# A planned order by longest path, more filling matmuls, and one matmul for a step of a recurrence

## The reference

```
attn_a: q,k,v = x@W_qkv.T + b;  gains = softmax(q@W_qscale.T + scale_gain)   # 16 heads of 8, 11 scales
        out += gains[j] * D4[tau] * sum(q * shift(k, d*tau)) * shift(v, d*tau)  # d = 1,2,4..., tau = 0..3
        out += softplus(bypass) * sum(q*k) * v;  result = (out * sigmoid(x@W_gate.T + b)) @ W_out.T + b_out
ffn:    e = argmax(x@Wg.T) of 8 experts;  y = gelu(x@W1[e] + b1[e]) @ W2[e] + b2[e]
attn_b: h = tanh(h@A.T + (x@B.T)[t]);  y[t] = h@C.T  for t = 0..511;  layernorm(y + x)*gamma + beta
ffn:    as above, with the same weights
```

## Time and profile before

| | us |
|---|---|
| median of the runs (3) | 1426.97 |
| lowest, highest run | 1420.13, 1428.18 |
| span of the profiled execution | 1436.4 |
| PE busy in it | 1170.8 (82%) |
| DVE, ACT, POOL busy | 796.3, 651.3, 788.6 |
| mean granted PE clock | 0.858 |

### The profile page before, as it was taken

The page is one execution under the profiler, slowest core; times in us unless marked ns, Lnnn a source line. Parts: engine busy times, 40 slices in busy tenths (PEclk is TensorE's granted clock), DMA queues, the critical chain, the costliest instruction groups (busy, mean ns, idle before and its releaser), DMA issues. The chain is left out here.

```text
span 1436.4 us, 32831 instructions
## 1 busy us (share of the span) xinstructions
PE 1170.8 (82%) x9942; PEld 881.1 (61%) x9942; DVE 796.3 (55%) x1723; ACT 651.3 (45%) x2050; POOL 788.6 (55%) x1274
## 2 busy tenths in 40 slices
PE   3877886888888899789988899887899998995580
PEld 2644554566565666466655666676787777785570
DVE  4878788889966777576788647542122301240110
ACT  2233332465544664455554436363564344562250
POOL 2645458563776748862748844876315642324504
PEclk9989987999988998889999759788995567998895
DMA  4700001221221212111112221233332324444542
GB/s 126 213 1 0 1 1 47 61 65 58 86 66 44 64 44 70 51 51 38 44 46 86 60 63 46 77 97 105 108 104 77 98 83 123 118 132 121 146 116 60
DMA packets 117638, 107.58 MB, mean 75 GB/s; under 512 B 15540, under 2 KB 88541, under 8 KB 117469
## 3 DMA queue, kind: packets, MB, share of 16 engines
q1 hardware_dynamic: 106704, 88.01, 21.5%
q0 software_dynamic: 8192, 16.79, 3.9%
q10 hardware_dynamic: 2573, 0.69, 0.2%
HBM read 76.73 MB, written 28.70 MB: 73 GB/s over the span
## 5 line engine op out<-in xcount | busy, mean ns | idle before, releaser
L799 POOL TENSOR_TENSOR acc<-acc,term 128x512 f32<-128x512 f32 x219 | 281.5, 1286 | 71.9 <-DVE term L1341 54.8
L1160 PE MATMUL bank<-w,hT 128*128 x1088 | 217.5, 324 | 22.1 <-ACT hT L985 13.9
L1341 DVE TENSOR_TENSOR term<-bank,V 128x512 f32<-128x512 f32 x251 | 168.0, 684 | 67.2 <-PE bank L1110 44.0
L1005 ACT ACTIVATE hid<-bank 128x16 f32<-128x16 f32 x512 | 93.0, 182 | 243.6 <-PE bank L1187 203.0
L985 ACT ACTIVATE hT<-bank,b1T 128x128 f32<-128x128 f32 x544 | 165.2, 370 | 79.2 <-PE bank L1147 65.2
L839 POOL DMA_INDIRECT back<-sorted_y,slot_i x128 | 125.1, 978 | 135.8 <-DMA back<-sorted_y,slot_i 44.2
L1160 PEld LDWEIGHTS bank<-w,hT 128*128 128x128 f32 x1088 | 173.9, 221 | 41.1 <-issue 35.6
L1187 PEld LDWEIGHTS bank<-hid,abcT 128*32 128x32 f32 x4096 | 88.6, 116 | 162.2 <-ACT hid L1005 83.2
L1312 DVE SCALAR_TENSOR_TENSOR made<-bank,qkvb,K 128x512 f32<-128x512 f32 x251 | 176.2, 742 | 17.8 <-PE bank L1083 7.2
L1187 PE MATMUL bank<-hid,abcT 128*32 128x16 f32 x4096 | 138.6, 201 | 38.3 <-ACT hid L1005 37.1
L1147 PE MATMUL bank<-xTb,w1b 128*128 128x128 f32 x864 | 166.8, 321 | 3.2 <-ACT xTb L973 3.0
(11 more groups left out here) (177 smaller groups left out, 2153.4 us busy)
## 6 DMA issues: line engine op xcount, KB each, us to landing
w1b<-in_W SPq DMA_DIRECT2D x130, 256.0 KB
K<-in_W SPq DMA_DIRECT2D x54, 256.0 KB
xsb<-sorted_x SPq DMA_DIRECT2D x184, 64.0 KB
sorted_y<-ysb SPq DMA_DIRECT2D x136, 64.0 KB
X<-in_x SPq DMA_DIRECT2D x64, 64.0 KB
out_x<-X SPq DMA_DIRECT2D x64, 64.0 KB
sorted_x<-K SPq DMA_DIRECT2D x14, 256.0 KB, 3.6
sorted_y<-made SPq DMA_DIRECT2D x48, 64.0 KB
```

What stands on the lines that cost most here:

```text
L799: nc.gpsimd.tensor_tensor(acc[:], acc[:] if k > 1 else term[0][:], term[k % NTERM][:], ALU.add).then_inc(S["terms_added"], 1)
L1005: nc.scalar.activation(hid[n % 2][:, cs], bank[6 + n % 2][:, cs], ACT.Tanh).then_inc(S["h_ready"], 1)
L1160: last = nc.tensor.matmul(bank[SLOT_BANK[place(n)]][:, 0:D], tile(hT[place(n)], c), w2[:, ds(second[n] + c * D, D)], start=(c == 0), stop= ...
L1341: V_.tensor_tensor(term[k % NTERM][:], bank[2 + k % 2][:], V[:, at:at + CW], ALU.mult).then_inc(S["terms_ready"], 1)
```

## The change

Three things change; the computation does not.

1. The planner's durations are replaced by pairs (how soon the engine can take the next piece, when the result is there), with a delay by pair of engines. The choice goes by the longest path that still hangs on a piece, instead of the earliest start.
2. The filling rule: every planned gap may be filled, at 0.11 us a matmul, as many as bring the planned columns of a stretch up to a target. There are 1916 fillers in place of 486, and bank 0 may take them too.
3. A step of the recurrence is one matmul of 128 rows.

```diff
-    def piece(engine, what, n, k, us, rank, after, lands=0.15, bank0=None):
-        us = us * PE_PACE if engine == "PE" else us
+PACE = dict(
...
+    rows=(0.42, 0.60), rxb=(0.93, 1.06), ry=(0.92, 1.06), step=(0.22, 0.33), turn=(0.12, 0.27), xT=(0.45, 0.60),
...
+    rnorm=(0.38, 0.48), rnorm2=(0.38, 0.48), xnorm=(0.38, 0.48), rcopy=(0.49, 0.58), rxcopy=(0.49, 0.60), state=(0.08, 0.18),
...
+HOP = {("ACT", "PE"): 0.13, ("ACT", "DVE"): 0.03, ("PE", "ACT"): 0.05, ("PE", "DVE"): 0.04, ("DVE", "PE"): 0.06, ("DVE", "ACT"): 0.03}
...
-            piece("PE", "step", c, k, 0.28, URGENT,
-                  [("state", c, k - 1) if k else past("state", c - 1, CT - 1), ("rxb", c, 0) if k == 0 else None])
+            piece("PE", "step", c, k, [("state", c, k - 1) if k else past("state", c - 1, CT - 1), ("rxb", c, 0) if k == 0 else None])
...
-                choice = (at, todo[key][2], ready, key)
...
+        to_go[key] = max((hop(todo, key, y) + to_go[y] for y in followers[key]), default=todo[key].took)
...
+            if r <= now + LOOK_US:
+                choice = (DAWDLE * max(0.0, r - now) - to_go[key], key)
...
+SPAN_US, TARGET, FILL_US, FILL_COLS, FREE_US = 3.4133, 6000, 0.11, 256, 0.3
...
-        if best and end and BEGIN[key] - best[0] > IDLE_US:
-            out[key] = int((BEGIN[key] - best[0]) * FILL_SHARE / FILL_US), best[1], best[2]
+        lack = TARGET - sum(c for _, c in recent) - columns_of(*key)
+        most = int((at - since) / FILL_US)
+        if end and lack > 0 and most > 0:
+            late = sum(since + FILL_US * j > stop - SPAN_US for j in range(most))
+            times = most - late + min(late, -(-lack // FILL_COLS))
...
-                    if reader:
+                    if reader and b == 0:
+                        pe.wait_ge(S["bank0_taken"], filled)
+                    elif reader:
...
-                    for q in range(4):
-                        last = nc.tensor.matmul(bank[6 + u][32 * q:32 * q + 32, k * NB:(k + 1) * NB],
-                                                abcT[:, 32 * q:32 * q + 32], prev, start=False, stop=True,
-                                                skip_group_check=True)
-                    last.then_inc(S["step_psum"], 1)
+                    nc.tensor.matmul(bank[6 + u][:, k * NB:(k + 1) * NB], abcT[:, 0:D], prev, start=False, stop=True,
+                                     skip_group_check=True).then_inc(S["step_psum"], 1)
```

More of the change, by code:

```diff
@@ new lines, in cost @@
+def cost(what, n, k):
+    if what in ("hidden", "result"):
+        us = 0.222 * HC / parts(n)
+        return us, us + 0.17
+    if what == "gelu":
+        us = 0.25 * HC / parts(n)
+        return us, us + 0.12
+    if what == "spread" and terms(n)[k].g not in (0, 1):
+        return 0.87, 1.02
+    if what == "spread":
+        return 0.31, 0.47
+    if what == "scale" and k == 2:
+        return 0.21, 0.31
+    if what == "xmom" and STATS_GROUP[n][1] - STATS_GROUP[n][0] == 1:
+        return 3.16, 3.17
+    return PACE[what]
@@ L192, in past, with pieces, piece @@
+def pieces():
+    todo = {}
+    def piece(engine, what, n, k, after, bank0=None):
+        todo[what, n, k] = Piece(engine, *cost(what, n, k), [x for x in after if x is not None], bank0)
     def past(what, n, k=0):
         return (what, n, k) if n >= 0 else None
-    URGENT, USUAL = 0.0, 1.0
     for i in range(CHUNKS):
@@ L282, in timeline @@
-        piece("DVE", "resid", i, 0, 0.7, USUAL, [("out", i, 0)], bank0=0)
+                piece("POOL", "add", i, j, [("term", i, j), ("add", i, j - 1) if j > 1 else None, past("out", before)])
+        piece("PE", "gatep", i, 0, [("xcopy", i, 0), past("gate", before)], bank0=1)
+        piece("ACT", "tanh", i, 0, [("gatep", i, 0)], bank0=0)
+        piece("DVE", "gate", i, 0, [("add", i, n - 1), ("tanh", i, 0)])
+        piece("PE", "out", i, 0, [("gate", i, 0)], bank0=1)
+        piece("DVE", "resid", i, 0, [("out", i, 0)], bank0=0)
@@ L359, in timeline @@
+        piece("PE", "rxb", c, 0, [("rxcopy", c, 0)])
         for k in range(CT):
[L360 to L365 removed]
@@ L376, in timeline @@
-    engines = ["SP", "POOL", "ACT", "PE", "DVE"]
-    left = {key: len(x[3]) for key, x in todo.items()}
+            piece("PE", "step", c, k, [("state", c, k - 1) if k else past("state", c - 1, CT - 1), ("rxb", c, 0) if k == 0 else None])
+            piece("ACT", "state", c, k, [("step", c, k), past("ry", c - 2) if k == 0 else None])
+        piece("PE", "ry", c, 0, [("state", c, CT - 1)])
+        piece("DVE", "rres", c, 0, [("ry", c, 0)])
+        piece("DVE", "rstats2", c, 0, [("rres", c, 0), past("rmom2", c - 2)])
@@ new lines, in pieces, with hop @@
+        piece("POOL", "rmom2", c, 0, [("rstats2", c, 0), past("rnorm2", c - 2, TPC - 1)])
+        for k in range(TPC):
+            piece("ACT", "rnorm2", c, k, [("rmom2", c, 0), ("rnorm2", c, k - 1) if k else None])
+        piece("DVE", "rgam", c, 0, [("rnorm2", c, TPC - 1)])
+        piece("DVE", "rbeta", c, 0, [("rgam", c, 0)])
+        piece("DVE", "rout", c, 0, [("rbeta", c, 0)])
+    return todo
+def hop(todo, x, y):
+    e, f = todo[x].engine, todo[y].engine
+    return todo[x].took + HOP_OF.get((x[0], y[0]), HOP.get((e, f), 0.08)) + LANDS.get(x[0], 0.0)
@@ L430, in fillings @@
+CLOSED_BY = dict(xT="xcopy", kproj="kcopy", vproj="vcopy", logit="shift", rows="rcopy", reduce2="pack2", gatep="tanh", out="resid",
+                 pT="pcopy", plog="plg", counts="ccopy")
 def fillings():
[L433 to L434 removed]
+    out, end, recent = {}, None, []
+    last_of = {b: None for b in range(8)}
     for key in ORDER["PE"]:
         what, n, k = key
+        at, stop = BEGIN[key], BEGIN[key] + WORK[key].pace
         best = None
[L438 to L439 removed]
+        for b, x in last_of.items():
+            since = max(end or at, BEGIN[x] + WORK[x].took + FREE_US) if x else end or at
```

314 lines of the change are left out of this document (162 added, 152 removed).

## The result

| | before | changed |
|---|---|---|
| median of the runs | 1425.43 (4 runs) | 1320.78 (4 runs, 1314.4 to 1323.52) |
| ratio to before, 95% interval | | 0.9285 [0.9224, 0.9346] |
| span of the profiled execution | 1436.4 | 1321.6 |
| mean granted PE clock | 0.858 | 0.950 |

A forecast was written before the change was run, and what follows sets the result against it. No engine is full; chains of small pieces waiting in in-order queues, chiefly the stream of slots, set the end. Terms -70 - 25 - 15 - 33 + 15 = -128 took 1427 to 1299 us, range 1195 to 1425.

The forecast's parts named there:

- order, waits and clock: Slots beside attention -70 us, PE's waits for states -25, the half-clock stretch of 19 slots behind attention -15.
- fillers: 1430 more matmuls in PE's gaps hold the clock: -10, -15 and -8 us in three stages, together -33.
- the step: One 128-row matmul per recurrence step: half of 16 us PE time, plus 7 us for later results, +15 us.
- a possible 140: Most the two stretches of 23 slots beside attention could save at the third's 5.3 us a slot: 81 and 59 us.
- my bound of 37: Most the half-clock stretch of 19 slots could save: 139 us down to 102 at 5.3 us a slot.
- My bound of 120: Most that PE's waits in front of states could return, from a row of 120.3 us in 161 waits.
- a microsecond at half clock in which PE sets the pace: Fillers' term: worth 0.4 us each, so at most 32, 52 and 26 us in three stages.
- Rival 3: Array shape costs on the way into a step too: step's term -8 instead of +15, 1276 us; chance 0.11.
- My estimate of 213 ns: Two weight loads of 128 columns by the skill's rule, near the 0.22 us forecast for a new step's hold.
- The signs given: Trace readings named beforehand to show the forecast right or wrong: slot stretches, state waits, clock, step timings, attention's end.
- Rival 1: The order returns nothing, since a better plan slips too; only fillers and step remain, 1409 us; chance 0.15.
- Rival 4: Recurrence put off into half clock: 267 steps behind attention's end at 1.66 us each, 1450 us; chance 0.12.

The follow-up runs named there:

- the pair of kernels on one chip: Kernel before with only the new filling rule, 1423.76 us, against the changed kernel with the old step of four 32-row matmuls, 1352.52 us.
- the first two kernels of the third chip: Changed kernel without the 447 fillers behind the last spread, 1402.88 us; changed kernel with its planner's step hold at 0.15 instead of 0.22 us, 1402.83 us.

## Why the prediction was right, and where it was not

The ledger predicted -110 for order, waits and clock, -33 for fillers, +15 for the step, -128 in all. Measured: order with its fillers -71 on one chip, step -32 against the changed kernel on others, together -103.

**Order: -70, -25 and -15 us, with -33 for fillers, measured -71 together.** Each mechanism is there, and in its own view larger than I took it. In the pair of kernels on one chip, the stretches of 23 slots beside attention are 98 us shorter from first to last transpose, of a possible 140. The 19 slots behind attention are 25 us shorter there; the 54 us of the result, over my bound of 37, compare with a trace that holds 11 us of "remote" waits and 92 us at half clock in this stretch, and the old order took 104 us for it, not 118, where those waits were missing. The wait for states fell by 61 us, counted once. My bound of 120 for it was wrong by its reading: the row of 120.3 us adds the waits of weight loads and of matmuls, which lie inside each other, so that 83 us was all there was. The last job, for which I took nothing from the order, gave 19 us. The end came forward by 71 us only. These are views of one chain of time, not separate savings: PE's waits are part of what made the slots long. Adding them to each other and to the fillers made the sum for order and fillers, 143 us, twice what was measured. That the sum of -128 came near -105 is in part luck: this overcount and the wrong sign of the step's term offset each other.

**Fillers: -33.** In the new order they are worth 46 us: 27 and 25 us in the first two stages (I took 10 and 15), and 1 and -4 in the others, where I took 8 for the last job. The 46 us are those of all 1916, while my -33 was for the 1430 that are new. In the old order more fillers are worth nothing beyond what the old 486 gave. I had put "a microsecond at half clock in which PE sets the pace" at 0.4 us; 356 us less at half clock (489 to 132) gave 46 us, 0.13 us each. That PE doesn't set the pace for most of it is the likely reason, not shown apart.

**Step: +15, measured -15 in the old order and -32 in the new one. This step of the prediction failed.** It said "A waiting piece adds about 0.1 us whatever its shape", since a transpose had the same 0.32 us before it as a step. The rows were right and the reading wrong. One more row of the kernel before, just ahead of that product, shows why:

```profile
1046.46 0.26 PE L1187 MATMUL bank<-hid,abcT 128*32 128x16 f32 x8
1046.65 0.49 PE L1160 MATMUL bank<-w,hT 128*128 x2
```

The product stood directly behind a step, and it was that which made it long. In the whole trace, at full clock, a product (L1147 or L1160) behind a step takes 0.325 us (median of 181), behind other work 0.223 us to the next product (562) and 0.223 us to a transpose (42), but 0.316 us to a step (190). So the 0.1 us ahead of a step was the price of its shape, and with the new step it is gone. Rival 3 named this mechanism and its sign; its price of 0.22 us for the step itself was too high (0.142 us measured), so it gave -8 where -32 came.
The Trainium skill's rule (TensorEngine Tiling, Key Properties) that changing the tiling mode drains TensorE agrees with the traces both ways, though it names no price: 0.094 us more on the way into 32-row matmuls, 0.10 us more on the way out of them (0.185 to full width for 0.084 to 32 rows), and 0.08 us more from the new full-width step to 32 rows than to full width.
My estimate of 213 ns for two weight loads, from the rule of the Trainium skill (TensorE: Matmul & The Clock Gate, LDWEIGHTS), does not hold as the time that a step among other work takes PE: 142 ns. It is near what a step that follows fillers takes, 0.23 us.

**The signs given.** Stretches of 23 slots under 170 us: 142 and 143. PE's wait for states under 80 us: 42.6 in that view, 33.8 counted once. Clock above 0.95 up to 446 us: 0.99. Step to state 0.40 us: 0.42 for a step behind a filler (1059.91 to 1060.33), but 0.32 at 542.96 us, where its weights were loaded ahead. Chunk 13's steps 0.65 us apart: 0.67. Step to the next piece 0.22 us: 0.14, the miss above. Attention's end before 930 us: 905; clock behind it over 0.7: 0.90 to 0.87. Rival 1 (order returns nothing) fell with the 71 us. Rival 4 did not happen here: from the last spread (869) the 267 steps took 295 us, 1.10 us each. Its picture, steps put off into a half clock, did appear in the kernel with two matmuls of 64 rows (435 us, 1.63 us a step).

## What to carry to other kernels

A small product of 32-row matmuls among full-width ones is paid for on the way in and on the way out: look at the start of the matmul before and of the one after, with and without it, before counting what the product itself takes. In a kernel of fixed lists, a longest-path choice needs accurate durations: on wrong ones it lost 73 us against the kernel before, and more fillers on an old list raised the clock and won nothing. What the longest path adds once the durations are right was not shown. When a view adds up an engine's waits, see whether it counts two queues that wait for the same thing. When kernels from different runs disagree, run the unchanged one beside them on the same chip, and look for waits that no instruction of the trace ends.

## What was not expected of the hardware

The order of pieces repeats between chips to a few us in 1320 (1320.78 and 1319.63 us), as long as a chip has no "remote" waits; with them the same list was 62 us later by 931 us. They come at the same places of a list: in the first two kernels of the third chip at 434, 478, 556 and 563 us, and 432, 476, 555 and 562 us. Nearly all fall where POOL issues its scatters and gathers. What gives them on some chips and not on others is open. And one matmul shape, 64 rows, that costs 0.04 us more than another went with a stretch of 436 us where every other kernel had 290 to 346: no run here shows what would have lifted the clock in it. The price of the array's shape, about 0.1 us each time it is entered or left, and the 0.08 us that a product loses behind any step, new or old, had not been expected either.
